# Cross-attention and FP4 feed-forward on one core: the context-by-weight product in two fp16 parts with one power of two per batch, and the loop bodies of four engines and of the SP queue in another order

## The reference, cut to what matters

```
q   = layernorm(x)                       # along D
t   = Wt @ ctx ; p = Wp @ q ; g = Wg @ ctx     # Wt, Wp, Wg: 256 x 256
att = sum(pg * gg) * 0.125               # one number per group
y   = Wz[group] @ (att * t)              # 32 x 32 per group
x1  = x + groupnorm(y) * gamma + beta + ctx
out = x1 + fp4_linear(silu(fp4_linear(n, w_gate)) * fp4_linear(n, w_up), w_down),  n = layernorm(x1)
```

## Time and profile before

| | us |
|---|---|
| runs (3) | 1738.07, 1738.39, 1740.09; median 1738.39 |
| profiled execution | 1737.87, its span 1736.0 |
| busy in the span: PE, DVE | 1680.2 (97%), 1506.6 (87%) |
| busy in the span: ACT, POOL | 825.9 (48%), 722.1 (42%) |
| granted TensorE clock, mean | 0.998 |

### The profile page before, as it was taken

How to read it: one execution, slowest core, us unless ns; L and a number is a source line. 1 busy time by engine, 2 the same in 40 slices (tenths; PEclk the granted TensorE clock), 3 DMA queues, 4 the chain that set the end, 5 groups by cost and what they waited for, 6 DMA issues and landing times.

```text
span 1736.0 us, 27880 instructions
## 1 busy us (share of the span) xinstructions
PE 1680.2 (97%) x8723; PEld 919.5 (53%) x8723; DVE 1506.6 (87%) x2577; ACT 825.9 (48%) x1472; POOL 722.1 (42%) x951
## 2 busy tenths in 40 slices
PE   2799999999999999999999999999999999999999
PEld 1665555555555555555555555555555555555544
DVE  7877888889888888988898898889888988888887
ACT  3665454544445444444545444454444444545322
POOL 7986343334444333344433334443333444433310
PEclk9999999999999999999999999999999999999999
DMA  8114334343434344343334434343434444433321
GB/s 258 34 43 86 81 91 92 88 100 89 98 77 94 89 93 98 85 106 74 89 89 100 93 88 101 76 92 91 99 88 97 92 84 91 93 90 88 76 53 47
DMA packets 412150, 155.86 MB, mean 90 GB/s; under 512 B 383200, under 2 KB 384480, under 8 KB 412128
## 3 DMA queue, kind: packets, MB, share of 16 engines
q1 hardware_dynamic: 396352, 125.17, 33.8%
q10 hardware_dynamic: 15776, 30.41, 5.5%
HBM read 43.03 MB, written 16.78 MB: 34 GB/s over the span
## 4 chain that ended last, share of the span: by engine, by line
PE 91%; POOL 6%; DVE 1%; DMA 1%; issue 1%; ACT 0%; SPq 0%; POOLq 0%; DVEq 0%; ACTq 0%
PE pairs L550 52%; PE work L561 25%; PE work L500 5%; PE work L512 3%; PE work L527 2%; PE ubank L527 2%; POOL raw L1863 2%; POOL raw L1852 1%; POOL w_parts L1863 1%; POOL w_parts L1852 1%; DMA raw<-in_L_ffn_w_gate 0%; DMA hT_parts<-raw 0%; POOL xc L1786 0%; PE pairs L580 0%; POOL q_parts L1802 0%
## 5 line engine op out<-in xcount | busy, mean ns | idle before, releaser
L550 PE MATMUL pairs<-w_gate_hi,xT_parts 128*128 128x512 f16 (+1 forms) x1536 | 555.4, 362 | 1.5 <-DMA xT_parts<-raw 1.5
L550 PE MATMUL pairs<-w_up_hi,xT_parts 128*128 128x512 f16 (+1 forms) x1536 | 554.7, 361 | 0.0
L561 PE MATMUL work<-w_parts,hT_parts 128*128 128x512 f16 x2079 | 458.9, 379 | 0.9 <-DMA hT_parts<-raw 0.9
L561 PEld LDWEIGHTS work<-w_parts,hT_parts 128*128 128x128 f16 x2079 | 203.6, 99 | 236.0 <-issue 1.1
L550 PE MATMUL pairs<-w_up_lo,xT_parts 128*128 128x512 f16 (+1 forms) x768 | 277.5, 361 | 0.0
L550 PE MATMUL pairs<-w_gate_lo,xT_parts 128*128 128x512 f16 (+1 forms) x768 | 277.4, 361 | 0.0
L550 PEld LDWEIGHTS pairs<-w_gate_hi,xT_parts 128*128 128x128 f16 x1536 | 152.7, 99 | 162.9 <-issue 14.6
L550 PEld LDWEIGHTS pairs<-w_up_hi,xT_parts 128*128 128x128 f16 x1536 | 150.3, 98 | 146.5
L964 ACT ACTIVATE early<-pairs,w_unit 128x512 f32<-128x512 f32 (+1 forms) x192 | 124.9, 650 | 163.5 <-PE pairs L550 163.4
L873 ACT CAST raw<-hq 128x704 f16<-128x704 f32 x126 | 98.1, 779 | 180.0 <-DVE hq L1201 179.3
L1409 DVE SCALAR_TENSOR_TENSOR h<-pairs,w_unit,early 128x512 f32<-128x512 f32 (+1 forms) x192 | 135.0, 703 | 39.9 <-ACT early L964 34.7
(11 more groups left out here) (193 smaller groups left out, 2799.8 us busy)
## 6 DMA issues: line engine op xcount, KB each, us to landing
out<-raw SPq DMA_DIRECT2D x64, 256.0 KB, 2.1
c_in<-in_ctx ACTq DMA_DIRECT2D x29, 512.0 KB, 3.8
x_in<-in_x ACTq DMA_DIRECT2D x29, 512.0 KB, 5.3
raw<-in_L_ffn_w_down SPq DMA_DIRECT2D x2, 1408.0 KB, 8.7
raw<-in_L_ffn_w_gate SPq DMA_DIRECT2D x2, 1280.0 KB, 8.4
...
```

The costliest lines, as they stand in the source:

```text
L550: mm = pe.matmul(pairs[:, pair, n, 0:b - a], xT[s][part][:, k, :], w1[n][wpart][:, k, a:b], start=(k == 0 and part == 0 and wpart == 0), s ...
L561: mm = pe.matmul(obank[:, :], hT[part][:, k, :], w2[wpart][:, k, :], start=(k == 0 and part == 0 and wpart == 0), stop=(k == KH - 1 and pa ...
```

## The change

The scale of the context becomes one power of two for the whole batch. `ctx_square` writes its squares into the new tile `c_scaled`; `save_rows` sends the 2 row sums of each partition to a DRAM tensor by a DMA from ACT's queue, `spread_rows` reads all 256 back onto every partition (`c_all`), and DVE's `ctx_peak` takes their maximum before `ctx_root`. `ctx_fit` now writes the fp16 part and the scaled fp32 context (4 instructions), `ctx_lo` on POOL subtracts them into the second fp16 part. `ctx_hi` and `ctx_fit_lo` go. `u_rows` multiplies fp16 by fp16 from `c_parts`; `copy_u` applies the inverse scale, which `scale_of_u` (DVE) makes. In the prologue `wuT` is scaled and split into fp16 on DVE after its own maximum has been to DRAM and back (`attention_peak`, two SP DMAs, `attention_parts`). The bodies of SP, PE, ACT, DVE and POOL are reordered.

```diff
-        wuT = [sb(f"wuT_{part}", [P, HT, C], F32R) for part in ("hi", "lo")]
+        wuT = [sb(f"wuT_{part}", [P, HT, C], F16) for part in ("hi", "lo")]
-        c_wide = [sb(f"c_{part}", [P, HT, D], F32R) for part in ("hi", "lo")]
+        c_scaled = sb("c_scaled", [P, HT, D])
+        c_all = sb("c_all", [P, HT * P])
...
@@ SP, prologue and body
+            wait_apart(sp, ident_made, wu_peaked, 1)
+            sp.dma_start(wu_rows, wu_pow[:, 0:1]).then_inc(wu_saved, 16)
+            sp.wait_ge(wu_saved, 16)
+            sp.dma_start(wu_all[:], wu_rows.rearrange("p n -> (p n)").unsqueeze(0).to_broadcast([P, P])).then_inc(wu_spread, 16)
...
                 turn_x(j + 1, 1)
-                if ahead:
-                    turn_c(i + 2)
                 store(j - 1, 1)
                 turn_h(j)
+                if more:
+                    turn_x(j + 2, 0)
                 if ahead:
                     turn_q(i + 2)
-                if more:
-                    turn_x(j + 2, 0)
+                    turn_c(i + 2)
                 store(j, 0)
@@ PE
-                pe.wait_ge(c_ready, HT * b + HT)
+                pe.wait_ge(c_fit_ready, HT * b + HT)
...
-                        mm = pe.matmul(u_bank(b, s), wuT[wpart][:, k, s * P:(s + 1) * P], c_wide[part][:, k, :],
+                        mm = pe.matmul(u_bank(b, s), wuT[wpart][:, k, s * P:(s + 1) * P], c_parts[:, k, part, :],
...
-                if more:
-                    gram(i + 1)
                 pe.wait_ge(x_turned, 16 * (j) + 16)
                 pe.wait_ge(h_done, GROUPS * (j - 1) + 2)
                 hidden(j, 0, 0)
                 if more:
-                    mixed(i + 1)
+                    gram(i + 1)
                     u_rows(i + 1, 0)
                     u_rows(i + 1, 1)
+                    mixed(i + 1)
@@ ACT
+            def save_rows(b):
+
+                act.wait_ge(c_squared, HT * b + HT)
+                at_least(act, c_rows_spread, 16 * b)
+                nc.scalar.dma_start(c_rows, c_norm[:, 0, :]).then_inc(c_rows_saved, 16)
+
+            def spread_rows(b):
+
+                act.wait_ge(c_rows_saved, 16 * b + 16)
+                at_least(act, c_peaked, b)
+                nc.scalar.dma_start(c_all[:], c_rows.rearrange("p h -> (p h)").unsqueeze(0).to_broadcast([P, HT * P])
+                                    ).then_inc(c_rows_spread, 16)
...
                 for s in range(HT):
                     nc.scalar.activation(c_parts[:, s, 0, :], c_in[:, s, :], ACT.Identity,
-                                         scale=c_norm[:, 2, s:s + 1]).then_inc(c_fit_done, 1)
...
+                                         scale=c_norm[:, 2, 0:1]).then_inc(c_fit_done, 1)
+                    nc.scalar.activation(c_scaled[:, s, :], c_in[:, s, :], ACT.Identity,
+                                         scale=c_norm[:, 2, 0:1]).then_inc(c_scaled_done, 1)
...
             ctx_square(0)
-            act.wait_ge(attw_split, 1)
+            save_rows(0)
             weight_grain(0)
+            spread_rows(0)
+            weight_grain(1)
             ctx_fit(0)
@@ DVE
+            def ctx_peak(b):
+
+                dve.wait_ge(c_rows_spread, 16 * b + 16)
+                at_least(dve, c_floored, b)
+                nc.vector.tensor_reduce(c_norm[:, 1, 1:2], c_all[:, :], AX_X, ALU.max).then_inc(c_peaked, 1)
...
+            def scale_of_u(b):
+
+                dve.wait_ge(c_inv_done, b + 1)
+                at_least(dve, u_copied, HT * b)
+                nc.vector.tensor_scalar(u_scale[:, 0:1], c_norm[:, 3, 0:1], wu_pow[:, 5:6], None,
+                                        ALU.mult).then_inc(u_scale_made, 1)
@@ POOL
             def ctx_root(b):
 
-                pool.wait_ge(c_squared, HT * b + HT)
+                pool.wait_ge(c_peaked, b + 1)
...
-                nc.gpsimd.tensor_tensor(c_wide[1][:, s, :], c_in[:, s, :], c_wide[0][:, s, :].bitcast(F32),
-                                        ALU.subtract).then_inc(c_ready, 1)
+                pool.wait_ge(c_fit_done, HT * b + s + 1)
+                pool.wait_ge(c_scaled_done, HT * b + s + 1)
+                nc.gpsimd.tensor_tensor(c_parts[:, s, 1, :], c_scaled[:, s, :], c_parts[:, s, 0, :],
+                                        ALU.subtract).then_inc(c_fit_ready, 1)
...
```

More of the change, by code:

```diff
@@ L1131, in body @@
                 if ahead:
-                    ctx_fit(i + 2)
+                    ctx_square(i + 2)
+                    save_rows(i + 2)
+                x_hi(j + 1)
                 silu_group(j, 0, 1)
-                x_hi(j + 1)
-                if ahead:
-                    ctx_hi(i + 2)
                 silu_group(j, 0, 2)
@@ L1497, in _ @@
             weight_unit(0)
+            weight_max(1, 1)
+            ctx_peak(0)
+            weight_round(0)
             ctx_power(0)
-            weight_max(1, 1)
-            weight_round(0)
+            attention_parts()
+            scale_of_u(0)
             weight_scales(1, 0)
@@ L1617, in body @@
                     sum_pg(i + 1, 0)
-                h_lo(j - 1, 0)
-                x_scales(j + 1)
-                x_y(j + 1)
+                x_add(j + 1)
+                x_back(j + 1)
                 if ahead:
-                    ln1_moments(i + 2, 0)
-                    ctx_power(i + 2)
-                gated(j, 0, 0)
+                    ln1_means(i + 2)
                 if more:
                     sum_pg(i + 1, 1)
+                h_lo(j - 1, 0)
+                gated(j, 0, 0)
                 h_lo(j - 1, 1)
-                x_add(j + 1)
-                x_back(j + 1)
                 if more:
@@ L1665, in body @@
                     normalise1(i + 2, 0)
+                h_lo(j, 1)
+                gated(j + 1, 1, 0)
+                if more:
+                    normalise2(j + 2)
+                if ahead:
+                    ctx_peak(i + 2)
                 if more:
                     x_first(j + 2)
+                    x_scales(j + 2)
+                    x_y(j + 2)
                 if ahead:
                     normalise1(i + 2, 1)
-                if more:
-                    x_scales(j + 2)
-                    x_y(j + 2)
-                gated(j + 1, 1, 1)
-                gated(j + 1, 1, 2)
-                h_first(j + 1)
+                    ctx_power(i + 2)
                 if more:
                     x_add(j + 2)
+                gated(j + 1, 1, 1)
+                if more:
                     x_back(j + 2)
                     x_quant(j + 2)
+                gated(j + 1, 1, 2)
+                if more:
                     x1_moments(j + 3)
                     x_lo(j + 2)
+                h_first(j + 1)
                 h_scales(j + 1, 1)
+                h_y(j + 1)
+                if ahead:
+                    scale_of_u(i + 2)
                 if more:
                     x1_mean(j + 3)
-                h_y(j + 1)
+                h_units(j + 1, 1)
                 emit(j, 0, 16 * i)
-                h_units(j + 1, 1)
             with dve.Fori(1, NB - 2) as i:
```

174 lines of the change are left out of this document (98 added, 76 removed).

## The result

The changed kernel takes 1950.13 us (median of 6 runs, 1944.89 to 1958.16) against 1738.36, a ratio of 1.1223 (95% interval 1.1197 to 1.1249): slower by 212 us where 54 were forecast. The profiled execution spans 1950.9 us.

The account below looks back on a forecast made before the run. TensorE's own work bounds the body (50.32 us). Body 1 + 0.46, bodies 2 to 30 29 x (52.0 - 50.32) = + 48.7, prologue + 5: + 54 on 1737.9 gives 1792 us; forecast's own range 1770 to 1815, overall 1727 to 1818.

Parts of the forecast that it names:

- u's matmuls: TensorE: the twelve matmuls of u as fp16 take 2.60 us instead of 3.00, 0.40 less a batch, bounds 0.3 to 0.5.
- Place 1: Before output(j-1): h_lo behind sum_pg makes the h transpose late, TensorE waits 0.86 us a body, bounds 0.4 to 1.2.
- Place 2: Before gram(i+1): the late context scale delays turn_c, gram waits 1.2 us; body 52.0 us, bounds 50.8 to 53.5.
- g: Time origin for place 2's count: start of the last gated of tile j on VectorE.
- case C: Rival: overlaps cost more and h_y pushes a POOL subtraction back; body 53.5 us, + 98, 1836 us; chance 0.11.
- From gram to the next g TensorE needs 16.9: TensorE's stages from gram to the next tile's last gated, summed from earlier stage lengths: 16.9 us.
- the prediction's own loop: Place 2's loop: landing at g + 35.1 plus 16.9 from gram to the next g, a body of 52.0 us.
- The overlap of VectorE and GpSimd: add_ctx beside h_snap_add and x_y: 0.56 us each, two such, 1.1 us later landing.
- The 52.7 by that rule: Body in us if both overlaps cost their full 0.93 and 0.88, landing at g + 35.8; not adopted.
- The prologue: Before the bodies: the first root waits for two DMAs and a reduction, + 5 us, bounds 3 and 10.
- Rival A: All lands in time, TensorE waits for nothing, if place 2's file is some 2 us shorter: 1729 us; chance 0.20.
- Rival C: The same as case C: body 53.5 us, + 98, 1836 us; chance 0.11.

Follow-up runs that it names:

- e12: A reordered variant (1812.6 us: mid-body context, early h_hi, load and emit) with h_hi(j-1) and h_lo(j-1) back at the changed kernel's late places: 1857.1 us.
- e1: The changed kernel with the context of batch i+2 made in the middle of the body, turn_c behind turn_h(j): 1889.5 us.
- e18: e17 with one move: GpSimd does both ctx_lo one behind the other, ahead of add_ctx(i+2,0): 1741.0 us, ratio 1.0014.
- e4: The changed kernel with 16 more matmuls of 512 columns on constants, between a body's first hidden group and gram: 1913.6 us.
- e16: New arithmetic with bodies in the earlier kernel's order (1781.7 us), plus the prologue's two maxima by TensorE instead of two DMA trips: 1774.9 us.
- e14: A reordered variant (1876.2 us) with the prologue's two maxima brought to all partitions by small TensorE matmuls instead of two DMA round trips: 1869.5 us.
- e7: A mid-body-context, early-h_hi variant (1847.5 us) with weight_y(2) ahead of the first root and weight_round(0) ahead of the first ctx_peak in the prologue: 1845.9 us.
- e11: A variant with early load and emit (1812.6 us), plus weight_y(2) ahead of the first root and weight_round(0) ahead of the first ctx_peak: 1809.8 us.
- e17: e16 with gated(j+1,1,0) ahead of normalise2(j+2), the spread ahead of grain_x(j+1), and weight_y(5) ahead of the second root: 1758.2 us.

## Why the prediction was wrong

- **Direction and places: right.** Slower; output(j-1) waits for hT, gram for cT, turn_c 1.9 us behind turn_q.
- **u's matmuls: right by themselves, too large in the sum.** 1041.96 - 1039.37 = 2.59 us, 2.60 predicted. But mixed ahead of them went from 1.54 to 1.73, so the net is 0.22 a batch, not 0.40. That is below the 0.3 of the bounds too. The first fp16 matmul behind mixed starts 0.19 later, as much as the first F32R one took more than the others before (0.42 against 0.23). The clean body is 50.08, not 49.92, which makes 5 us over the run.
- **Place 1: right mechanism, mis-sized.** 0.86 predicted, 1.3 of wait on average (39.9 / 30), 1.53 a body by e12. The landing took 6.4 us in the body shown, not 5.2. turn_x went out at 1012.75, while it ran; whether that is why wasn't tried.
- **Place 2, the landing of turn_c: this is the step that failed.** Forecast g + 35.1, measured g + 38.4 in the body shown. The snap (2.21 us) and x_y (1.47) beside add_ctx made x_quant end 1.4 later than without overlaps, where 1.1 had been counted, so they are only 0.3 of the miss. x_hi stood 0.7 behind q's cast, which the prediction had at nothing. q_lo was held 1.4 behind h_y, which it had put into case C. The landing took 5.3 instead of 4.3 (medians 5.7 and 4.3): turn_c goes out 1.9 behind turn_q, and in e1 and e18, where the two stand apart or in the other order, it is 4.3 again. The busy share of the DMA engines doesn't tell the two cases apart: 0.81 here, 0.89 in the 7.5 us behind turn_c in e18. Over the run TensorE waited 3.5 us a time (102.8 / 29) where 1.2 had been forecast.
- **"From gram to the next g TensorE needs 16.9": false after a wait, and not among my cases at all.** This is the second step that failed. The prediction had TensorE's matmuls behind a wait at their length at full clock, so it priced a wait at the wait alone. From 994.29 to 1014.18 it took 19.9 us, gram alone 5.30 instead of 2.78. Of 29 grams behind an idle time of 1.9 to 4.3 us, 23 took 4.2 to 5.3 us and six 2.79. With both parts put in, the prediction's own loop is 38.5 + 19.9 = 58.4; that is the measured body split in two, and no test of the loop. A mean body of 57.2 has 3.5 us of wait before gram, 1.3 before output(j-1) and some 2.1 of slower matmuls on the 50.1 of e18, 57.0 in all. Against the forecast 52.0 that is 2.3 more of the first wait, 0.4 of the second, 0.2 for u and the 2.1 of slower matmuls, which had been put at nothing. e4 shows that the clock follows from the idle time. The Trainium skill, TensorE: Matmul & The Clock Gate, section "Part 1: The HAM clock gate", says that the clock of the array depends on how busy it has been recently; by that rule, the trace agrees (0.50 behind the idle time above). I had not applied it to a stall that I forecast myself.
- **The overlap of VectorE and GpSimd: priced too low, but a small part.** The prediction took 0.56 of the earlier trace rows for each of two overlaps. The snap beside add_ctx gained 0.59 for 0.72 us in common and x_y 0.78 for 0.92, together 1.4 instead of 1.1. Normalise2 in e16 gained 0.84, the three of e1 2.87 beside ctx_lo and add_ctx. By the time in common that is 82 and 85%, where 0.56 for 0.93 and 0.88 was 60 and 64%. The rule of the Trainium skill (SBUF — State Buffer, "Who interferes with whom"), full exclusion, is nearer by that share, though the snap's 0.59 itself is what the earlier trace rows said. The 52.7 by that rule would still have been far off, because of the clock.
- **The prologue: direction right, size wrong.** + 5 predicted, + 18.7 measured. The save took 7.0 and the spread 3.5 us, I had 4.5 and 3; the root came at 32.6, not 29.4. The 2 us for one DMA, which stand beside the prediction's lower bound, held for neither. That accounts for about 7 (e14). What the other 12 us are isn't settled. The order of the weights' steps among the new ones is the suspect: one exchange on GpSimd and one on VectorE, made together, gave 1.6 us in e7 and 2.8 in e11. With one exchange more (e17, not priced by itself) e18 is left with 9.3.
- **Rival A** asked for a file 2 us shorter; e18 shows that a clean body exists for this arithmetic, in the old order of TensorE. **Rival C** named the subtraction pushed by h_y, and at its right size (1.5, measured 1.4); its + 98 is still less than half of the 212, since it had no slower matmuls either.
